# A selective scan over 24-slot passes: skip products behind the side jobs, copies of y a slot later, and a backward convolution ahead of the sums

## The chip, the cores and the metric

One core of a Trainium2 chip runs the whole program. The metric is device time in microseconds. The kernel before was run three times, with a median of 18989.68 us.

## The reference

The model has two layers over x, 16 images of 192 channels and 56 x 56 = 3136 positions. Each layer adds its branch to x: `x = x + branch(gn(x))`. The first is a bidirectional RWKV recurrence and isn't touched. The second, where the change is, is a bidirectional selective scan:

```python
def _branch(x, conv_w, conv_b, W_xproj, W_dt, dt_bias, A_log, D):
    xc = silu(conv_b + sum((xp[:, k:k + L, :] * conv_w[:, k] for k in range(4))))
    dbl = xc @ W_xproj.T
    dt = softplus(dbl[..., :12] @ W_dt.T + dt_bias)
    Bc, Cc = dbl[..., 12:28], dbl[..., 28:]
    A = -exp(A_log)
    # h = h * exp(dt * A) + (dt * x) * B;  y = sum over the 16 states of h * C;  + x * D
    return _selective_scan(xc, dt, Bc, Cc, A, D)

x, z = layernorm(tok) @ W_in_x.T, layernorm(tok) @ W_in_z.T      # 192 -> 384 channels
y_f = _branch(x, forward weights)
y_b = _branch(x[:, ::-1, :], backward weights)[:, ::-1, :]
out = ((y_f + y_b) * silu(z)) @ W_out.T + b_out
```

All is float32. The skip term is `x * D` in the scan.

## The kernel before, in words

A loop runs over the 16 images. Each round has one block for the first layer and one for the second, and only the second matters here.

**Tiling.** The 3136 positions are cut into seven chunks of 448. The second layer goes over them forwards (passes 0 to 6) and then backwards (passes 7 to 13); the 384 channels are three groups of 128 (`e` or `k` = 0, 1, 2), and the 16 states are taken in eight pairs (`p` = 0 to 7). One slot is one pair of one group, so a pass has 24 slots and an image 336. In a slot `q` these instructions carry the recurrence:

- ScalarE makes the decays exp(dt * A) in PSUM (L1410, twice), sets the state between the two halves (L1419) and keeps the carried state (L1427).
- VectorE (odd pairs, L1252) or GpSimd (even pairs, L1471) makes the input products du * B.
- VectorE scans (L1263).
- GpSimd multiplies the scan's output by C (L1479). Its results lie in a ring of four buffers, and the output product of slot q waits until the sum of slot q - 4 is done. The scan's results lie in a ring of three, and the scan of slot q waits for the output product of slot q - 3.
- TensorE adds the products up into y, in one PSUM bank (`YBANK`): in each odd slot the sums of two slots (L1157, four matmuls), two slots behind the scan. The first matmul into y of each group is the skip product `skipd` (L1149), which starts the accumulation anew, so the former y must have been read by then (`y_free`).

y is read by a copy on ScalarE in forward passes (`ye`, L1375; SyncE then stores it in DRAM, `ys`, L1561) and by a product with the gate on VectorE in backward passes (`ye`, L1239). In backward passes L1152 adds the stored forward y.

**Side jobs.** What prepares the next pass runs in the gaps: the normalization (`ns`, `n1`, `n2`, `nm`), the projection (`x` on TensorE, L1081, copied by ScalarE, `xe`, L1329), the causal convolution (`cv`, four matmuls, L1095), its silu in four steps on ScalarE (`c1` to `c4`: L1336, L1341, L1345, L1349) with the last product on VectorE (`xc`, L1226), the projections `xp` (L1102) and `t` (L1107, step size; read by L1363 on ScalarE), and in backward passes the gate (`z`, L1112, read by L1382 and released by `z4`, L1399) and the output projection (`o`, L1134, read by `ou`, L1244). `dp` (L1062) spreads du for VectorE's products.

**What sets the order.** `side_schedule` writes for each engine a list of times in slots, one for each side job; sorted by time, they give the order. An engine does the side jobs of slot g (those with time below g + 1) at the end of its slot g. The times only order the work within an engine; what makes engines wait is semaphores. For a backward pass the convolutions have the times `1.3, 6.0, 10.7` after `t = PER * (i - 1) - 2.5`, so that of group 0 falls in slot 22 of pass i - 2, group 1's in slot 3 (3.5) and group 2's in slot 8 (8.2). The preparation of pass i lies in the slots of pass i - 1; passes 6 to 12 prepare the seven backward ones.

The same function gives each TensorE job one of the banks 6 and 7 (`WBANK`), the one that is released first by the times:

```python
b = banks[k % len(banks)] if t < -10 else min(banks, key=lambda n: until.get(n, -99))
until[b] = release[name, i, e]
jobs[name, i, e] = (k, b, used.get(b, 0))
```

A job waits until all former uses of its bank are released (`w.wait_ge(c_wf[b], n)`). With this rule the convolutions of groups 0 and 1 of a backward pass follow one another on the same bank (pass 10: both bank 7, uses 55 and 56; pass 11: both bank 6, uses 59 and 60). A convolution's bank is released by `xc` (L1226) on VectorE, for group 0 in slot 3 (3.4), behind the scan and the input product of that slot. The banks are the same before and after the change.

TensorE's main loop has, in each slot, first the skip product (if the slot begins a group), then the sums (if it is odd), then the side jobs.

Of the kernel before, what the change touches and what calls it, by code (L numbers as in the profile page):

```python
# [24 lines left out]
Q = NI * PER  # L25
CHUNK = [(0, c) for c in range(NC)] + [(1, c) for c in reversed(range(NC))]
# [13 lines left out]
NXC, NDT, NDU, NR2 = 5, 3, 3, 3  # L40
# [24 lines left out]
def side_schedule():  # L65


    pe, act, dve, pool, sp = [], [], [], [], []

    def conv(i, e, t):  # L70
        if (i, e) == (0, 0):
            dve.append((t, "cd", i, e))
        else:
            pe.append((t, "cv", i, e))
        act.extend([(t + 1.9, "c1", i, e), (t + 2.6, "c2", i, e), (t + 3.2, "c3", i, e), (t + 3.9, "c4", i, e)])
        dve.append((t + 4.6, "xc", i, e))

    def step_size(i, e, t):
        pe.append((t, "t", i, e))
        act.extend([(t + 1, "t1", i, e), (t + 2, "t2", i, e), (t + 2.6, "t3", i, e)])  # L80
        dve.append((t + 2.9, "td", i, e))
        pool.append((t + 3.9, "du", i, e))
        pe.append((max(NP * (EJ * i + e) - 2, t + 4.5), "dp", i, e))
        o = max(t + 3.4, NP * (EJ * i + e - 2) - 0.5 if i else t)
        sp.extend([(o, "dd", i, e), (o + 0.02, "de", i, e), (t + 5 if i or e else o + 0.01, "ud", i, e)])

    def project(i, t, u, v):

        pe.append((t, "xp", i, 0))
        act.append((t + v, "p1", i, 0))  # L90
        sp.append((t + 1.5, "cw", i, 0))
        for e in range(EJ):
            step_size(i, e, t + u[e] if i or not e else (-1.9, 1)[e - 1])
        for G in range(4):
            r = PER * i - NP + 2 * G if i else -100
            if i:
                sp.extend([(max(r + 1, t + 2), "bl", i, G), (max(r + 3, t + 2.1), "cl", i, G)])
            else:
                sp.extend([(t + (5.3 if G else 2) + G, "bl", i, G), (t + 5.9 + G, "cl", i, G)])

    def gate(i, e, t):
        pe.append((t, "z", i, e))
        act.extend([(t + 2, "z1", i, e), (t + 2.7, "z2", i, e), (t + 3.3, "z3", i, e), (t + 4, "z4", i, e)])
        pool.append((t + 4.8, "g", i, e))

    for i in range(NI):
        s = CHUNK[i][0]
        t = PER * (i - 1) - 2.5 * (i > 1) if i else -60
        if not s:
            act += [(t - 1.7, "ns", i, 0)]  # L110
            dve += [(t + 1.0, "nc", i, 0)]
            pe += [(t - 0.2, "n1", i, 0), (t + 2.1, "n2", i, 0)]
            act += [(t + 1.9, "nq", i, 0), (t + 3.0, "nr", i, 0), (t + 4.6, "xh", i, 0)]
            if i:
                pool += [(t + 3.4, "nm", i, 0)]
            else:
                dve += [(t + 1.9, "nq", i, 0), (t + 3.4, "nm", i, 0)]
            sp += [(t + 5, "nw", i, 0), (t + 8, "xw", i, 0)]
            for e, (u, v) in enumerate(((4.2, 6.4), (4.3, 8.6 if i > 1 else 7.4), (6.2, 11))):
                pe.append((t + u, "x", i, e))  # L120
                act.append((t + u + 1.2, "xe", i, e))
                conv(i, e, t + v)
            project(i, t + 15.6, (1.2, 1.7, 4.7), 1.2)
        else:
            sp += [(t - 8, "xl", i, 0), (t + 9, "nl", i, 0)]
            for e, v in enumerate((1.3, 6.0, 10.7)):
                conv(i, e, t + v)
            project(i, t + 15.6, (1.9, 2.3, 5.2), 1.5)
            t += 2.5
            gate(i, 0, t + 21.6)  # L130
            gate(i, 1, t + 26.4)
            gate(i, 2, t + 33.4)
            for k in range(CJ):
                o = t + 2 * PER + (6.4, 7.9)[k]
                pe.append((o, "o", i, k))
                dve.append((o + 1.5, "ou", i, k))
            sp.append((o + 2.5, "out", i, 0))
            sp.append((t + PER + 4, "yl", i, 0))
        for e in range(EJ):
            t = NP * (EJ * i + e + 1) + LAG - 1  # L140
            if not s:
                act.append((t + 0.9, "ye", i, e))
            else:
                dve.append((t + 1.5, "ye", i, e))
        if not s:
            sp.append((t + 1.5, "ys", i, 0))
    sp += [(PER * (NC - 2) + 13, "dg", 1, 0), (PER * (NI - 2) + 13, "dg", 0, 0)]
    sp.append((PER * NC, "pl", NI - 1, 0))
    dve += [(PER * (i + 2) + 12 if i < NI - 2 else Q - 9, "st", CHUNK[i][1], 0) for i in range(NC, NI - 1)]
    dve += [(PER * 9 + 20, "st", 0, 0), (Q - 8.5, "ga", 0, 0), (Q - 6.5, "gb", 0, 0), (Q - 2.5, "gd", 0, 0)]  # L150
    pe += [(Q - 7.5, "gm", 0, 0), (Q - 4.5, "gv", 0, 0), (Q - 1.5, "gw", 0, 0), (Q + 0.2, "oa", NI - 1, 0),
           (Q + 0.3, "oa", NI - 1, 1), (Q + 9, "gk", 0, 0)]
    act += [(Q - 5.5, "gq", 0, 0), (Q - 3.5, "ge", 0, 0), (Q - 3.4, "gs", 0, 0), (Q - 0.5, "gi", 0, 0)]
    plans = [sorted(p, key=lambda a: a[0]) for p in (pe, act, dve, pool, sp)]
    jobs, used, until = {}, {}, {}
    last = dict(n1="nc", n2="nr", x="xe", cv="xc", xp="p1", t="td", z="z4", o="ou", gm="gi")
    read = {(name, i, e): t for p in plans[1:4] for t, name, i, e in p}
    release = {(name, i, e): read.get((last.get(name), i, e)) for _, name, i, e in plans[0]}
    for k, (t, name, i, e) in enumerate(a for a in plans[0] if a[1] not in ("dp", "gv", "gw", "gk", "oa")):
        banks = WBANK if t >= -10 else [*WBANK, 0, 1, 2, 3]  # L160
# [3 lines that stand above are left out]
        used[b] = used.get(b, 0) + 1  # L164
        if t < -10:
            first = dict(used)
    jobs["cv", 0, 0] = (None, DUBANK, 0)
    return plans, jobs, first
# [19 lines left out]
def build(nc, d, ctx):  # L188
    def sb(name, shape, dt=F32):
        return ctx.enter_context(nc.sbuf_tensor(name, shape, dt))  # L190
# [24 lines left out]
    skipd = sb("skipd", [128, 2, EJ, 128])  # L215
# [269 lines left out]
    def take(*shape, parts=128, phase=None):  # L485

        if phase is not None:
            at[0] += (phase - at[0]) % 4
        n = 1
        for s in shape:  # L490
            n *= s
        o = at[0]
        at[0] += n
        assert at[0] <= arena_n, at[0]
        v = arena[0:parts, o:o + n]
        if len(shape) == 2:
            v = v.rearrange("p (a b) -> p a b", a=shape[0])
        elif len(shape) == 3:
            v = v.rearrange("p (a b c) -> p a b c", a=shape[0], b=shape[1])
        return v  # L500
# [19 lines left out]
    ys = take(NU, T)  # L520
# [431 lines left out]
    xc = take(NXC, T, phase=0)  # L952
# [47 lines left out]
    def freed(w, name, i, e=0):  # L1000

        _, b, k = jobs[name, i, e]
        w.wait_ge(c_wf[b], k + 1)
# [30 lines left out]
    def y_free(w, r):  # L1034

        w.wait_ge(c_ya, min(r, EJ * NC))
        w.wait_ge(c_yv, r - EJ * NC)

    def layer1_tensor(e):
        w = Waits(e)  # L1040
# [100 lines left out]
        for g in range(-2, Q + LAG):  # L1141
            q = g - LAG
            if 0 <= q < Q:
                r, i, k, p, s = pair(q)
                y = ps[:, YBANK, 0:T]
                if p == 0:
                    y_free(w, r)
                    freed(w, "cv", i, k)
                    e.matmul(y, skipd[:, s, k, :], xc[:, r % NXC, :], start=True, stop=False)  # L1149
                if s and p == NP - 1:  # L1150
                    w.wait_ge(s_yl[i % 2], 16 * ((i - NC) // 2 + 1))
                    e.matmul(y, ident[:, :], yf[:, k, :], start=False, stop=False)  # L1152
                if p % 2:
                    w.wait_ge(c_mc, q + 1)
                    for a in range(2):
                        for h in range(2):
                            m = e.matmul(ps[64 * h:64 * h + 64, YBANK, 0:T], rep[:, 0:64],  # L1157
                                         pr[:, (q - 1 + h) % NPR, a * T:a * T + T], start=False,
                                         stop=p == NP - 1 and a == 1)
                            if a:  # L1160
                                m.then_inc(c_sm, 1)
            side(g)
        side(Q + 200)

    def layer1_vector(e):
# [501 lines left out]
```

## Time and profile before

| what | us |
|---|---|
| median of three runs | 18989.68 |
| lowest and highest | 18980.05, 19108.81 |
| the profiled execution | 19009.29 |
| its span, first to last instruction | 19007.5 |

Mean granted clock of TensorE: 0.885 of full speed. The trace is one execution. L12 is line 12 of the kernel, the idle time of an instruction is that of its engine just ahead of it, and the releaser is what the semaphores show as the last thing it waited for. All rows below are of the ninth image; the other fifteen repeat it closely.

### The profile page before, as it was taken

What the parts mean: (1) busy time and instruction counts of PE and PEld (TensorE: products, weight loads), DVE (VectorE), ACT (ScalarE), POOL (GpSimd) and SP (SyncE); (2) the same over time, 40 slices, a digit from 0 to 9 for tenths busy, and PEclk for the clock granted to TensorE, in tenths of its full rate; (3) what the DMA queues carried; (4) which work ended last, traced back from release to release, by engine and by line L of the source; (5) the groups of instructions that cost most, each with busy time, mean ns of one, the idle gap of its engine ahead of it and who ended that gap; (6) DMA issues with size and microseconds to landing.
All of it is one profiled execution on the core that took longest, in us unless ns stands there. A gap on an engine that the chain in (4) does not pass through costs nothing. (4 is left out here: it accounts for less than half of the span.)

```text
span 19007.5 us, 189410 instructions
## 1 busy us (share of the span) xinstructions
PE 15391.1 (81%) x45218; PEld 5361.0 (28%) x45218; DVE 17199.8 (90%) x13477; ACT 13152.4 (69%) x33212; POOL 16875.4 (89%) x11028
## 2 busy tenths in 40 slices
PE   7887888878888788887888878878788887888878
PEld 2222222322223222222222222222222222222222
DVE  7989989899898998989989899898998989989899
ACT  6767767677676776767767677676776767767676
POOL 6979979799797997979979799797997979979799
PEclk8988888888888888888888898888888889888888
DMA  2424424244242442424424244242442424424243
GB/s 74 121 60 114 120 63 120 60 115 119 67 118 61 114 117 67 118 66 112 114 67 118 66 116 110 67 118 65 114 113 67 119 68 116 108 68 121 70 117 103
DMA packets 880507, 1820.79 MB, mean 96 GB/s; under 512 B 189546, under 2 KB 595012, under 8 KB 879236
## 3 DMA queue, kind: packets, MB, share of 16 engines
q1 hardware_dynamic: 879236, 1807.12, 36.5%
q8 instruction: 398, 6.52, 0.1%
q14 instruction: 873, 7.15, 0.1%
HBM read 1083.80 MB, written 245.63 MB: 70 GB/s over the span
## 5 line engine op out<-in xcount | busy, mean ns | idle before, releaser
L1263 DVE TENSOR_TENSOR_SCAN arena<-ps,arena 128x897 f32<-128x897 f32 x5376 | 10993.9, 2065 | 521.1 <-ACT arena L1427 265.9
L1479 POOL TENSOR_TENSOR arena<-arena 128x896 f32<-128x896 f32 x5376 | 9418.8, 1769 | 311.2 <-DVE arena L1263 279.0
L1410 ACT ACTIVATE ps<-arena,A 128x448 f32<-128x448 f32 x10752 | 6390.9, 627 | 2360.2 <-DVE arena L1263 2277.1
L1157 PE MATMUL ps<-arena,rep 128*64 128x448 f32 x21504 | 5489.8, 641 | 1473.0 <-POOL arena L1479 1463.8
L1471 POOL TENSOR_TENSOR arena<-arena 128x896 f32<-128x896 f32 x2688 | 4770.4, 1775 | 202.5 <-DMA arena<-arena 131.4
L1252 DVE TENSOR_TENSOR arena<-ps,arena 128x896 f32<-128x896 f32 x2688 | 2867.0, 1067 | 69.3 <-PE ps L1062 63.3
L1157 PEld LDWEIGHTS ps<-arena,rep 128*64 128x64 f32 x21504 | 1484.1, 154 | 5086.2 <-POOL arena L1479 2720.6
L1095 PE MATMUL ps<-arena,diag 128*128 128x448 f32 x5248 | 2177.1, 559 | 77.6 <-DVE arena L1226 77.6
L1149 PE MATMUL ps<-arena,skipd 128*128 128x448 f32 x1344 | 823.7, 700 | 767.5 <-DVE arena L1239 645.7
L1095 PEld LDWEIGHTS ps<-arena,diag 128*128 128x128 f32 x5248 | 980.9, 194 | 1255.6 <-issue 1057.8
L1460 POOL TENSOR_TENSOR arena<-arena 128x448 f32<-128x448 f32 x672 | 656.3, 982 | 512.8 <-DVE arena L1232 512.8
L1427 ACT ACTIVATE arena<-arena 128x2 f32<-128x2 f32 x5376 | 1022.6, 190 | 40.9 <-DVE arena L1263 40.9
L1107 PE MATMUL ps<-arena,wdt 13*128 13x448 f32 x1344 | 751.5, 666 | 306.7 <-DVE arena L1232 295.2
L1419 ACT ACTIVATE arena<-arena 128x1 f32<-128x1 f32 x4608 | 867.8, 188 | 0.0
L1062 PE MATMUL ps<-arena,rep 64*128 64x448 f32 x1344 | 720.1, 618 | 151.1 <-DVE arena L1252 94.1
L922 POOL TENSOR_TENSOR arena<-arena 128x448 f32<-128x448 f32 x336 | 350.9, 1044 | 529.1 <-DVE arena L698 492.4
L1226 DVE SCALAR_TENSOR_TENSOR arena<-ps,vece,arena 128x448 f32<-128x448 f32 x672 | 449.7, 669 | 300.3 <-ACT arena L1349 300.3
L1336 ACT ACTIVATE arena<-ps,vece 128x448 f32<-128x448 f32 x672 | 420.9, 626 | 412.6 <-PE ps L1095 410.8
L308 PE MATMUL ps<-x,ws 96*128 96x448 f32 x1348 | 657.7, 624 | 45.7 <-DVE arena L714 45.6
L1081 PE MATMUL ps<-arena,wx 96*128 96x448 f32 x1344 | 590.8, 580 | 126.2 <-POOL arena L1454 115.9
L727 DVE TENSOR_TENSOR_SCAN ps<-ps,arena 128x898 f32<-128x898 f32 x336 | 680.3, 2025 | 11.9 <-ACT ps L885 10.3
L1112 PE MATMUL ps<-arena,wz 96*128 96x448 f32 x1344 | 668.4, 626 | 0.0
(181 smaller groups left out, 18857.7 us busy)
## 6 DMA issues: line engine op xcount, KB each, us to landing
arena<-bc_rows SPq DMA_DIRECT2D x3584, 224.0 KB, 4.5
arena<-arena SPq DMA_DIRECT2D x4160, 112.0 KB, 3.4
x_projected<-arena SPq DMA_DIRECT2D x112, 672.0 KB, 3.5
y_forward<-arena SPq DMA_DIRECT2D x112, 672.0 KB, 5.6
arena<-x_projected SPq DMA_DIRECT2D x112, 672.0 KB, 4.8
arena<-y_forward SPq DMA_DIRECT2D x112, 672.0 KB, 6.1
x<-in_x SPq DMA_DIRECT2D x120, 336.0 KB, 3.6
x_normed<-arena SPq DMA_DIRECT2D x112, 336.0 KB, 4.9
```

Of the source, the lines that this page charges most:

```text
L1062: e.matmul(ps[:, DUBANK, 0:T], rep[64:128, :], du[64:128, r % NDU, :], start=True, stop=True).then_inc(c_dp, 1)
L1095: m = e.matmul(o, diag[:, k, q, :], xh[i % 2][:, k, h:h + T], start=q == 0, stop=q == 3)
L1107: e.matmul(o, wdt[s][:, k * 128:(k + 1) * 128], res[0:R + 1, :], start=True, stop=True).then_inc(c_wt, 1)
L1149: e.matmul(y, skipd[:, s, k, :], xc[:, r % NXC, :], start=True, stop=False)
L1157: m = e.matmul(ps[64 * h:64 * h + 64, YBANK, 0:T], rep[:, 0:64], pr[:, (q - 1 + h) % NPR, a * T:a * T + T], start=False, stop=p == NP - 1 ...
L1252: e.tensor_tensor(two(bb[:, q % NB, :]), ps[:, DUBANK, 0:T].unsqueeze(1).to_broadcast([128, 2, T]), br[:, p - 1:p + 1, :], ALU.mult).then_ ...
L1263: e.tensor_tensor_scan(rev(hh[:, q % NH, 0:W2], s), rev(decays(q)[:, 0:W2], s), rev(bb[:, q % NB, 0:W2], s), car[:, 2 * k + p % 2, n:n + 1 ...
L1410: e.activation(two(decays(q))[:, a, :], dt2[:, r % NR2, p % 2, :], ACT.Exp, scale=Am[s][:, 2 * k + p % 2, n:n + 1]).then_inc(c_ex, 1)
L1419: e.activation(bb[:, q % NB, T:T1], car[:, 2 * k + p % 2, n:n + 1] if i % NC else zero[:, 0, 0:1], ACT.Copy).then_inc(c_rs, 1)
L1427: e.activation(car[:, 2 * k + p % 2, n:n + 2], h[:, 0:T1 + 1:T1] if s else h[:, T - 1:W2:T1], ACT.Copy).then_inc(c_ca, 1)
L1471: e.tensor_tensor(two(bb[:, q % NB, :]), du2[:, r % NR2, :].unsqueeze(1).to_broadcast([128, 2, T]), br[:, p:p + 2, :], ALU.mult).then_inc( ...
L1479: e.tensor_tensor(pr[:, q % NPR, :].rearrange("p (a b) -> p a b", a=2), two(hh[:, q % NH, :]), cr[:, p - p % 2:p - p % 2 + 2, :], ALU.mult ...
```

## The change

There are three parts.

1. The copy of y in forward passes and its store stand one slot later (`ye` from t + 0.9 to t + 1.9, `ys` from t + 1.5 to t + 2.5). The copy of x of group 2 (`xe`) and the first silu step of group 0 (`c1`) go one slot later with it.
2. TensorE's skip product, with its wait for y and for `xc`, stands at the end of its slot, behind the side jobs.
3. The backward convolution of group 1 has the time 2.8 in place of 3.5: slot 2, and so, by part 2, ahead of the skip product of slot 2 and of the sums of slot 3.

```diff
         else:
-            pe.append((t, "cv", i, e))
-        act.extend([(t + 1.9, "c1", i, e), ...
+            pe.append((t - 0.7 * (CHUNK[i][0] and e == 1), "cv", i, e))
+        act.extend([(t + 1.9 + 0.25 * (i > 0 and not CHUNK[i][0] and not e), "c1", i, e), ...
...
-                act.append((t + u + 1.2, "xe", i, e))
+                act.append((t + u + (2.2 if i and e == 2 else 1.2), "xe", i, e))
...
-                act.append((t + 0.9, "ye", i, e))
+                act.append((t + 1.9, "ye", i, e))
...
-            sp.append((t + 1.5, "ys", i, 0))
+            sp.append((t + 2.5, "ys", i, 0))
...
                 y = ps[:, YBANK, 0:T]
-                if p == 0:
-                    y_free(w, r)
-                    freed(w, "cv", i, k)
-                    e.matmul(y, skipd[:, s, k, :], xc[:, r % NXC, :], start=True, stop=False)
...
             side(g)
+            if 0 <= q < Q and p == 0:
+                y_free(w, r)
+                freed(w, "cv", i, k)
+                e.matmul(y, skipd[:, s, k, :], xc[:, r % NXC, :], start=True, stop=False)
```

TensorE, slots 2 to 5 of a backward pass, before. `wz` is the gate's product z, `diag` the convolution, `rep` the sums, `skipd` the skip product; c_ybwd is counted up by L1239, c_mulc by GpSimd's output products, c_free6 and c_free7 by the readers of the banks.

```order
L1149 MATMUL ps<-arena,skipd 128x448 [waits c_ybwd]
L1112 MATMUL ps<-arena,wz 128x448 [waits c_free6]
L1112 MATMUL ps<-arena,wz 128x448
L1157 MATMUL ps<-arena,rep 64x448 [waits c_mulc]
L1157 MATMUL ps<-arena,rep 64x448 x3
L1095 MATMUL ps<-arena,diag 128x448 [waits c_free7]
L1095 MATMUL ps<-arena,diag 128x448 x3
L1157 MATMUL ps<-arena,rep 64x448 [waits c_mulc]
L1157 MATMUL ps<-arena,rep 64x448 x3
```

The same place after the change (the lines of the sums and of the skip product have other numbers there, L1153 and L1162):

```order
L1112 MATMUL ps<-arena,wz 128x448 [waits c_free6]
L1112 MATMUL ps<-arena,wz 128x448
L1095 MATMUL ps<-arena,diag 128x448 [waits c_free7]
L1095 MATMUL ps<-arena,diag 128x448 x3
L1162 MATMUL ps<-arena,skipd 128x448 [waits c_ybwd]
L1153 MATMUL ps<-arena,rep 64x448 [waits c_mulc]
L1153 MATMUL ps<-arena,rep 64x448 x3
L1153 MATMUL ps<-arena,rep 64x448 [waits c_mulc]
L1153 MATMUL ps<-arena,rep 64x448 x3
```

The convolution has gone ahead of the skip product and of the first sums, and the skip product behind z.

ScalarE, slots 9 and 10 of a forward pass, before. L1375 is the copy of y, L1410 the decays, L1349 the last silu step of group 1, L1336 the first of group 2.

```order
L1345 ACTIVATE arena<-arena 128x448 [waits c_cexp]
L1375 ACTIVATE arena<-ps 128x448 [waits y_stored,c_sum]
L1410 ACTIVATE ps<-arena,A 128x448 [waits c_scan]
L1410 ACTIVATE ps<-arena,A 128x448
L1419 ACTIVATE arena<-arena 128x1 [waits c_carry]
L1427 ACTIVATE arena<-arena 128x2
L1349 ACTIVATE arena<-arena 128x448 [waits c_cln]
L1336 ACTIVATE arena<-ps,vece 128x448 [waits c_du,c_job]
```

The same place after:

```order
L1345 ACTIVATE arena<-arena 128x448 [waits c_cexp]
L1410 ACTIVATE ps<-arena,A 128x448 [waits c_scan]
L1410 ACTIVATE ps<-arena,A 128x448
L1419 ACTIVATE arena<-arena 128x1 [waits c_carry]
L1427 ACTIVATE arena<-arena 128x2
L1349 ACTIVATE arena<-arena 128x448 [waits c_cln]
L1336 ACTIVATE arena<-ps,vece 128x448 [waits c_du,c_sum,c_job]
L1375 ACTIVATE arena<-ps 128x448 [waits y_stored,c_sum]
```

The copy has moved behind the next decays and both silu steps. The orders of VectorE and GpSimd don't change. On SyncE the store of y goes behind one other store in each forward pass.

## Rows read from the trace of the kernel before

**Rows 1.** Windows, passes 3, 10, 12: us; busy (count) PE, PEld, DVE, ACT, POOL; PEclk; DMA

```profile
9951.41:10019.22 67.81, 55.13 (x161) 18.23 (x160) 64.56 (x45) 50.20 (x132) 66.87 (x42) 0.86 0.43 113
...
10427.10:10498.49 71.39, 59.27 (x175) 20.76 (x174) 67.04 (x51) 51.00 (x134) 67.66 (x43) 0.88 0.44 113
...
10568.38:10636.62 68.24, 56.58 (x176) 19.02 (x174) 66.83 (x51) 50.87 (x134) 67.74 (x43) 0.90 0.48 122
```

**Rows 2.** Waits of GpSimd (total us, times, longest): passes 8 to 12, then 2 to 5

```profile
POOL arena L1479 <- DVE arena L1263: 8.7, 11, 1.4
POOL arena L1479 <- PE ps L1157: 1.6, 2, 0.8
...
POOL arena L1479 <- DVE arena L1263: 3.4, 4, 0.9
```

**Rows 3.** Timeline of pass 3, slots 9 to 12: start, us, engine, line, [idle before]

```profile
9978.36 1.72 PE L1157 MATMUL ps<-arena,rep 128*64 128x448 f32 x8
...
9980.16 0.54 ACT L1375 ACTIVATE arena<-ps 128x448 f32<-128x448 f32 x1 [3.71 <-PE ps L1157]
...
9982.50 0.68 DVE L1226 SCALAR_TENSOR_TENSOR arena<-ps,vece,arena 128x448 f32<-128x448 f32 x1 [2.43 <-ACT arena L1349]
...
9985.26 1.76 POOL L1479 TENSOR_TENSOR arena<-arena 128x896 f32<-128x896 f32 x1 [0.83 <-DVE arena L1263]
...
9987.08 1.67 PE L1157 MATMUL ps<-arena,rep 128*64 128x448 f32 x4 [3.65 <-POOL arena L1479]
```

**Rows 4.** Timeline of pass 10, TensorE, slots 2 and 3

```profile
10434.69 1.86 PE L1149 MATMUL ps<-arena,skipd 128*128 128x448 f32 x2 [2.86 <-DVE arena L1239]
10436.35 3.19 PE L1112 MATMUL ps<-arena,wz 96*128 96x448 f32 x4
10439.47 2.56 PE L1157 MATMUL ps<-arena,rep 128*64 128x448 f32 x8
10441.96 3.27 PE L1095 MATMUL ps<-arena,diag 128*128 128x448 f32 x8
```

**Rows 5.** Timeline of pass 10, VectorE and ScalarE, slots 3 to 7

```profile
10437.54 0.67 DVE L1226 SCALAR_TENSOR_TENSOR arena<-ps,vece,arena 128x448 f32<-128x448 f32 x1
...
10445.27 0.64 ACT L1336 ACTIVATE arena<-ps,vece 128x448 f32<-128x448 f32 x1 [2.80 <-PE ps L1095]
...
10447.75 2.08 DVE L1263 TENSOR_TENSOR_SCAN arena<-ps,arena 128x897 f32<-128x897 f32 x1 [2.60 <-ACT arena L1427]
```

**Rows 6.** Timeline of pass 10, GpSimd: the fifth and sixth output products

```profile
10442.69 3.48 POOL L1479 TENSOR_TENSOR arena<-arena 128x896 f32<-128x896 f32 x2
```

**Rows 7.** Timeline, pass 10, slot 18; windows behind waits of 3.65, 2.86, 4.78 us

```profile
10484.40 1.86 PE L1149 MATMUL ps<-arena,skipd 128*128 128x448 f32 x2 [4.78 <-DVE arena L1239]
...
9987.00:9990.00 3.00, 2.92 (x8) 0.92 (x9) 3.00 (x2) 1.56 (x5) 3.00 (x3) 0.54 0.01 3
...
10434.60:10441.00 6.40, 6.31 (x10) 2.38 (x12) 6.40 (x6) 3.81 (x11) 6.40 (x6) 0.50 0.35 123
10484.40:10492.00 7.60, 7.60 (x16) 2.47 (x18) 6.90 (x4) 4.24 (x12) 7.60 (x7) 0.50 0.85 206
```

**Rows 8.** Timeline of pass 12, TensorE, slot 2; the window behind its wait

```profile
10575.98 1.02 PE L1149 MATMUL ps<-arena,skipd 128*128 128x448 f32 x2 [2.98 <-DVE arena L1239]
10576.83 1.67 PE L1112 MATMUL ps<-arena,wz 96*128 96x448 f32 x4
...
10575.90:10582.00 6.10, 6.02 (x19) 2.60 (x20) 6.10 (x6) 3.87 (x11) 6.10 (x5) 1.00 0.50 155
```

**Rows 9.** Timeline: passes 6 and 12, VectorE's L1226, GpSimd's fifth output product

```profile
10164.53 0.68 DVE L1226 SCALAR_TENSOR_TENSOR arena<-ps,vece,arena 128x448 f32<-128x448 f32 x1
...
10169.65 3.49 POOL L1479 TENSOR_TENSOR arena<-arena 128x896 f32<-128x896 f32 x2
...
10578.81 0.68 DVE L1226 SCALAR_TENSOR_TENSOR arena<-ps,vece,arena 128x448 f32<-128x448 f32 x1
...
10584.18 3.48 POOL L1479 TENSOR_TENSOR arena<-arena 128x896 f32<-128x896 f32 x2
```

More of the change, by code:

```diff
@@ L73, in conv @@
         else:
-            pe.append((t, "cv", i, e))
-        act.extend([(t + 1.9, "c1", i, e), (t + 2.6, "c2", i, e), (t + 3.2, "c3", i, e), (t + 3.9, "c4", i, e)])
+            pe.append((t - 0.7 * (CHUNK[i][0] and e == 1), "cv", i, e))
+        act.extend([(t + 1.9 + 0.25 * (i > 0 and not CHUNK[i][0] and not e), "c1", i, e), (t + 2.6, "c2", i, e), (t + 3.2, "c3", i, e), (t + 3.9, "c4", i, e)])
         dve.append((t + 4.6, "xc", i, e))
```

## Prediction, made before the changed kernel was run

> **What bounds the kernel now.** I read the windows view first, with image nine of sixteen cut into its 14 passes of 24 slots (at the first scan of each). A forward pass takes 67.8 us with GpSimd busy for 66.9 and VectorE for 64.6; a backward one 71.4 with 67.7 and 67.0; the last backward one that still prepares a successor 68.2 with 67.7 and 66.8 [rows 1]. So GpSimd (L1479, L1471) is packed, VectorE almost so, and no order of work takes a pass below some 67 us. The most that this change can give back is GpSimd's idle time. The waits view puts it at 10.3 us in five backward passes (8.7 for VectorE's scan, 1.6 for TensorE's sums) and 3.4 us in four forward ones, once 0.85 us in each [rows 2]. TensorE's and ScalarE's idle time counts only where one of these two waits for it.
>
> **Part 1, forward: copies of y one slot later.** The chain is read in pass 3 [rows 3]. ScalarE comes to the copy of y (L1375) and waits 3.71 us for the sums that TensorE starts at 9978.36; the decays and the last activation of the convolution (L1349) are queued behind it. VectorE therefore waits 2.43 us for L1349 before L1226, the next scan is late, and GpSimd loses 0.83 us. After the change the decays, L1349 and L1336 are ahead of the copy. The copy itself can't run before 9980.1 in either order, and its reader, the skip product, is needed only before the sums of the following odd slot. TensorE waits 3.65 us for GpSimd soon after those anyway, so the later copy is covered. The 2.43 us goes. What is late next is GpSimd itself, so each forward pass gains the 0.83, not the 2.43: 0.84 x 5 passes = 4.2 us per image. For the first pass, which starts without a predecessor and isn't in these rows, I take 1.3 us, between 0 and 4 (four such chains). The moved L1329, L1336 and the store of y on SyncE's queue (past one store of the normalized input) I cost at 0: ScalarE is idle for 17 us of each forward pass [rows 1], and the next user of the stored y comes seven slots later. If that cover were missing, a loss of up to the 0.84 of each pass would come back. Sum: -5.5 us per image.
>
> **Part 2, backward: skip product behind the side jobs.** In pass 10 TensorE waits 2.86 us for VectorE's L1239 in front of L1149, and z's products, the sums and the convolution all stand behind it; then they run with nearly doubled durations [rows 4]. ScalarE waits 2.80 us for that convolution, and the scan behind it 2.60 us [rows 5]. That stall is what opens GpSimd's idle time a few slots later. With L1149 moved, z's products (L1112) start as soon as the previous sums end, at 10431.83 (2.86 us before L1149's start), and at the full clock's 1.67 us [rows 8] are through at about 10433.5. In the second slot of this kind (a wait of 4.78 us [rows 7]) the moved step-size product frees ScalarE in the same way. GpSimd doesn't wait there, so I price this at 0, at most 0.7 us of VectorE's lead per pass.
>
> **Part 3, one backward convolution ahead of the sums.** Here the change costs. The planner gives the convolutions of channel groups 0 and 1 of a backward chunk the same bank, so group 1's must wait until VectorE's L1226 has read group 0's. That read stands in slot 3. Until now the convolution was in slot 3 too, behind the sums, and TensorE was late, so the wait hardly showed. Now it is in slot 2. In pass 10 L1226 ends at 10437.54 + 0.67 = 10438.21 [rows 5]; z's products end at 10433.5. So TensorE waits about 4.7 us, and behind the waiting matmul stand the skip product and the sums of pairs 0 and 1, which start at 10439.47 today and could start as soon as GpSimd's second output product is there. Who waits for these sums: GpSimd has four buffers for its output products, so its fifth one of the pass needs sum 0. It starts at 10442.69 [rows 6], which is 4.48 us after L1226's end.
>
> How long after L1226's end is the first sum done? At full clock: convolution 3.27 [rows 4], skip 1.02 [rows 8], sums 1.72 [rows 3], less 0.2 in which the runs overlap: 5.8 us. The clock decides the rest. After the wait of 2.86 us the granted clock was 0.50 (1.2 GHz) for 6.4 us; after the wait of 4.78 us, 0.50 for 7.6 us; after one of 3.65 us, 0.54 for 3 us; after one of 2.98 us in pass 12 it stayed at 1.00 (2.4 GHz) [rows 3, 7, 8]. The new wait of 4.7 us is near the longest of these, so I expect half clock behind it. Each us at half clock costs half a us: 3 us of it give 7.3, 5 us 8.3, 8 us 9.8. I take 5 us, the middle of what followed the two waits above 3.5 us (3 and 7.6), hence 8.3; the end at 8 us is rival D.
>
> GpSimd's fifth output product starts between 4.4 and 5.6 us after L1226's end in the seven passes 6 to 12, 4.8 in the mean; the first and the last of the seven are shown (4.44 and 4.69) [rows 9]. So GpSimd gets a new wait of 8.3 - 4.8 = 3.5 us in each of seven passes: 24.5 us per image. VectorE's lead can move L1226 ahead by some 0.3 us (its scan of slot 2 needs a GpSimd product and has little room): -2. The new wait stands ahead of the slots in which GpSimd idles now, so that idle time is absorbed, except for some 0.3 us per pass: 10.3 - 1.5 = 8.8 us go. Parts 2 and 3 together: 24.5 - 2 - 8.8 = +13.7 us per image.
>
> This rests on matmuls not overtaking one another, which the rows show in every slot. The Trainium skill (TensorE: Matmul & The Clock Gate, Step-by-step) says that only weight loads are pulled ahead, the matmuls staying in program order. If they could pass, the sums would run during the wait, and the sum would be that of rival C.
>
> **The sum.** +13.7 - 5.5 = +8.2 us per image, x 16 = +131 us. The profiled execution took 19009.29 us (its span is 19007.5), 19.6 above the median of the runs, 18989.68. Against its own time: 19140; put on the runs' median: 19120 us, 0.7% slower. A measurement of this kernel can tell about 1%.
>
> **Rivals.**
> B, the clock stays full. For it speaks pass 12 [rows 8], against it that its wait was only 2.98 us. Then 5.8 - 4.8 = 1.0 us x 7 = 7, less 2, less 8.8, less 5.5: -9.3 us per image, -149 us: 18840.
> C, the convolution's wait isn't there or isn't on GpSimd's path. What is removed counts alone: -(8.8 + 5.5) x 16 = -229 us: 18760, 1.2% faster. Against it: the bank and the rows above. For it: how far GpSimd runs ahead may shift once VectorE is relieved. If its fifth output product came 3.5 us later relative to L1226, nothing would be lost; this is the point from which C decides.
> D, half clock for the whole stretch (8 us, near the 7.6 of [rows 7]). Then 9.8 - 4.8 = 5.0 us x 7 = 35, less 2, 8.8 and 5.5: +18.7 us per image, +299 us: 19290, 1.6% slower. The skill's same page (HAM oscillation) describes this pattern, a wait in each round that makes each burst start cold. The trace agrees at 4.78 us and not at 2.98.
>
> **How the numbers follow.** Forecast 0.45 (19120), B 0.20, C 0.12, D 0.23. The range, 18890 to 19270, reaches nearly to B and to D. Faster by over 1% (below 18800): most of C, 0.10. Slower by over 1% (above 19180): D, and the upper third of the forecast's own spread (6 us at half clock instead of 5 adds 56 us), 0.37. Within 1%: 0.53.
>
> **What would show it.** Right: in passes 6 to 12 TensorE waits some 4 to 5 us before L1095 for VectorE's L1226, about 112 times; GpSimd's L1479 waits for TensorE's sums by 300 to 400 us in all; passes 6, 7 and 12 grow by 3 us each, passes 2 to 5 shrink by 0.8; ScalarE's waits at L1375 and VectorE's 2.43 us before L1226 are gone. Wrong: if passes 6 and 7, where GpSimd has no idle time to give back, keep their length, then part 3 costs nothing and C holds. If the wait before L1095 is there but the granted clock behind it is near 1, it is B.

## The result, and the profile after

| | before | after |
|---|---|---|
| device time, median of 6 runs each (us) | 19001.32 | 19174.34 |
| lowest to highest (us) | 18980.05 to 19108.81 | 19162.44 to 19180.65 |
| profiled span (us) | 19007.5 | 19172.4 |

The changed kernel is slower by 0.86% (ratio 1.0086, 95% interval 1.0073 to 1.01), 173 us. The forecast was 19120 us, the range 18890 to 19270. It stood on the first three runs of the kernel before (18989.68); of the 54 us between forecast and result 12 lie in that base and 42 in the change itself.

First the passes, from the windows view of after: image nine, passes 3, 6, 7, 10, 12 and 13, each from its first scan to the next pass's, the last to its last scan. Columns: stretch and length in us; busy time (count) of PE, PEld, DVE, ACT and POOL; granted clock; DMA share; GB/s.

```profile
10032.48:10100.05 67.57, 53.99 (x166) 18.35 (x164) 64.56 (x46) 50.69 (x132) 67.57 (x43) 0.90 0.45 114
10231.81:10296.16 64.35, 46.88 (x147) 15.47 (x146) 63.19 (x43) 46.58 (x121) 64.35 (x39) 0.89 0.45 115
10296.16:10365.03 68.87, 53.40 (x161) 18.46 (x160) 63.69 (x45) 51.20 (x135) 67.07 (x43) 0.90 0.49 125
10509.06:10579.86 70.80, 56.82 (x172) 20.05 (x170) 66.85 (x51) 51.28 (x134) 66.74 (x42) 0.90 0.44 113
10651.36:10722.95 71.59, 57.50 (x176) 19.90 (x176) 67.13 (x50) 51.20 (x134) 67.80 (x43) 0.90 0.46 117
10722.95:10790.41 67.46, 48.05 (x161) 16.02 (x160) 62.56 (x49) 40.05 (x110) 63.55 (x39) 0.80 0.20 50
```

Against [rows 1]: pass 3 has no GpSimd idle time left (67.57 of 67.57, with one instruction more in the stretch than before), while pass 12 grew from 68.24 to 71.59 with the same GpSimd work (67.74 and 67.80). Pass 10, which had idle time to give back, stayed at about 71.

Next the waits, over the whole run, of the kernel before (engine, line, what it waited for: total us, times, longest):

```profile
ACT arena L1375 <- PE ps L1157: 470.2, 187, 4.2
DVE arena L1226 <- ACT arena L1349: 300.3, 128, 4.5
POOL arena L1479 <- DVE arena L1263: 279.0, 318, 2.9
PE ps L1095 <- DVE arena L1226: 77.6, 112, 2.3
DVE x L1244 <- PE ps L1134: 36.3, 75, 1.1
POOL arena L1479 <- PE ps L1157: 21.9, 28, 0.8
```

and of the changed kernel (its sums are on L1153, not L1157):

```profile
PE ps L1095 <- DVE arena L1226: 397.6, 130, 4.7
POOL arena L1479 <- PE ps L1153: 353.6, 129, 3.9
DVE arena L1226 <- ACT arena L1349: 105.9, 48, 4.5
POOL arena L1479 <- DVE arena L1263: 92.7, 179, 2.2
ACT arena L1375 <- PE ps L1153: 87.1, 100, 1.1
DVE x L1244 <- PE ps L1134: 61.6, 32, 2.8
```

GpSimd's wait for VectorE's scan shrank by 186 us, and its wait for TensorE's sums grew by 332. The second outweighs the first. Two other rows moved: the convolution's wait for L1226 (78 to 398 us) and VectorE's for the output projection (36 to 62).

Then one place, slots 2 to 5 of pass 10. TensorE's timeline after the change, beside [rows 4]:

```profile
10511.72 1.72 PE L1153 MATMUL ps<-arena,rep 128*64 128x448 f32 x8 [1.11 <-POOL arena L1479]
10513.72 1.77 PE L1112 MATMUL ps<-arena,wz 96*128 96x448 f32 x4 [0.27 <-ACT arena L1399]
10520.22 5.78 PE L1095 MATMUL ps<-arena,diag 128*128 128x448 f32 x8 [4.73 <-DVE arena L1226]
10525.84 0.92 PE L1162 MATMUL ps<-arena,skipd 128*128 128x448 f32 x2
10526.68 3.23 PE L1153 MATMUL ps<-arena,rep 128*64 128x448 f32 x16
```

VectorE's and GpSimd's, of the same stretch:

```profile
10519.50 0.67 DVE L1226 SCALAR_TENSOR_TENSOR arena<-ps,vece,arena 128x448 f32<-128x448 f32 x1
10530.57 2.08 DVE L1263 TENSOR_TENSOR_SCAN arena<-ps,arena 128x897 f32<-128x897 f32 x1 [3.46 <-POOL arena L1479]
...
10528.57 3.49 POOL L1479 TENSOR_TENSOR arena<-arena 128x896 f32<-128x896 f32 x2 [3.90 <-PE ps L1153]
```

And the granted clock behind that wait (windows view, columns as above):

```profile
10520.00:10525.00 5.00, 4.78 (x7) 2.30 (x8) 5.00 (x4) 2.89 (x8) 4.67 (x3) 0.50 0.02 7
10525.00:10529.00 4.00, 4.00 (x19) 1.50 (x19) 2.11 (x2) 2.96 (x8) 0.43 (x1) 0.96 0.02 4
```

The reader sees one chain. z's products end at 10515.5. TensorE waits 4.73 us for L1226, which ends at 10520.17. The convolution then takes 5.78 us where [rows 4] had 3.27, since the clock is at 0.50 (1.2 GHz); the clock is back near 2.4 GHz only from 10525 on. The sums stand behind it, GpSimd's fifth output product waits 3.90 us for the first of them, and VectorE's next scan 3.46 us for GpSimd. From the end of L1226 to the fifth product it is 10528.57 - 10520.17 = 8.4 us.

### The profile page after: what moved, and what is told of

Its sections match the earlier page's. It is cut to its first block and busy times, and to the rows that moved or that the text cites. A ratio compares the mean times of both kernels' runs of the same rounds, so it can differ in the third digit from the quotient of the medians.

```text
span 19172.4 us, 189410 instructions
## 1 busy us (share of the span) xinstructions
PE 15559.6 (81%) x45218; PEld 5442.1 (28%) x45218; DVE 17204.9 (90%) x13477; ACT 13215.8 (69%) x33212; POOL 16867.6 (88%) x11028
## 5 line engine op out<-in xcount | busy, mean ns | idle before, releaser
L1479 POOL TENSOR_TENSOR arena<-arena 128x896 f32<-128x896 f32 x5376 | 9421.5, 1773 | 448.5 <-PE ps L1153 353.6
L1410 ACT ACTIVATE ps<-arena,A 128x448 f32<-128x448 f32 x10752 | 6396.1, 627 | 2979.8 <-DVE arena L1263 2895.4
L1153 PE MATMUL ps<-arena,rep 128*64 128x448 f32 x21504 | 5400.8, 631 | 1554.5 <-POOL arena L1479 1551.9
L1153 PEld LDWEIGHTS ps<-arena,rep 128*64 128x64 f32 x21504 | 1458.7, 151 | 5126.3 <-POOL arena L1479 2606.4
L1095 PE MATMUL ps<-arena,diag 128*128 128x448 f32 x5248 | 2402.3, 606 | 397.6 <-DVE arena L1226 397.6
L1095 PEld LDWEIGHTS ps<-arena,diag 128*128 128x128 f32 x5248 | 1072.3, 212 | 1697.7 <-issue 1185.4
L1162 PE MATMUL ps<-arena,skipd 128*128 128x448 f32 x1344 | 804.0, 685 | 501.8 <-DVE arena L1239 262.3
L1460 POOL TENSOR_TENSOR arena<-arena 128x448 f32<-128x448 f32 x672 | 659.1, 988 | 514.6 <-DVE arena L1232 514.5
L1107 PE MATMUL ps<-arena,wdt 13*128 13x448 f32 x1344 | 705.2, 629 | 261.8 <-DVE arena L1232 250.3
L922 POOL TENSOR_TENSOR arena<-arena 128x448 f32<-128x448 f32 x336 | 337.1, 1003 | 503.6 <-DVE arena L698 456.2
L1336 ACT ACTIVATE arena<-ps,vece 128x448 f32<-128x448 f32 x672 | 422.4, 629 | 515.3 <-PE ps L1095 511.8
L1081 PE MATMUL ps<-arena,wx 96*128 96x448 f32 x1344 | 655.0, 633 | 146.3 <-POOL arena L1454 137.0
L727 DVE TENSOR_TENSOR_SCAN ps<-ps,arena 128x898 f32<-128x898 f32 x336 | 680.1, 2024 | 11.9 <-ACT ps L885 10.3
L826 ACT ACTIVATE arena<-ps 128x448 f32<-128x448 f32 x336 | 181.9, 541 | 715.5 <-PE ps L310 220.2
L933 POOL TENSOR_TENSOR arena<-arena 128x448 f32<-128x448 f32 x336 | 349.6, 1040 | 361.0 <-ACT arena L872 360.9
```

Of the source, the lines that this page charges most:

```text
L1095: m = e.matmul(o, diag[:, k, q, :], xh[i % 2][:, k, h:h + T], start=q == 0, stop=q == 3)
L1107: e.matmul(o, wdt[s][:, k * 128:(k + 1) * 128], res[0:R + 1, :], start=True, stop=True).then_inc(c_wt, 1)
L1410: e.activation(two(decays(q))[:, a, :], dt2[:, r % NR2, p % 2, :], ACT.Exp, scale=Am[s][:, 2 * k + p % 2, n:n + 1]).then_inc(c_ex, 1)
L1479: e.tensor_tensor(pr[:, q % NPR, :].rearrange("p (a b) -> p a b", a=2), two(hh[:, q % NH, :]), cr[:, p - p % 2:p - p % 2 + 2, :], ALU.mult ...
```

## The experiments

Theory A says that the loss is part 3's wait for the shared bank, with all that is queued behind it. Its rivals say that another part brings it, or that the wait alone costs and the clock is a side effect. Each variant was run beside fresh runs of the kernel before, whose medians were 18999 to 19017 us, so the ratios compare variants better than the times do. Lengths below are means over 16 images from scan to scan, summed over passes; "rest" is from an image's last scan to the next image's first. The table is of one execution of each kernel; those of part 1 and of part 2 alone took 56 and 33 us more than the medians of their kernels (3.5 and 2.0 us per image).

| us per image | before | after | parts 1+2 | part 3 | part 1 | part 2 | dummies | last pass | early release |
|---|---|---|---|---|---|---|---|---|---|
| passes 0 to 5 | 418.7 | 411.7 | 411.9 | 420.8 | 413.2 | 419.9 | 412.0 | 412.2 | 412.3 |
| pass 6 | 64.4 | 64.2 | 64.4 | 64.7 | 64.4 | 64.8 | 64.2 | 64.2 | 64.0 |
| passes 7 to 12 | 417.1 | 428.6 | 407.7 | 412.2 | 416.2 | 407.4 | 413.3 | 407.7 | 408.6 |
| pass 13 | 63.1 | 67.4 | 65.9 | 63.8 | 63.3 | 65.3 | 66.0 | 64.2 | 65.0 |
| rest | 221.6 | 223.6 | 224.1 | 221.9 | 223.5 | 226.7 | 223.5 | 224.5 | 224.2 |

**Parts 1 and 2 without part 3.** The changed kernel with the convolution back behind the sums:

```diff
-            pe.append((t - 0.7 * (CHUNK[i][0] and e == 1), "cv", i, e))
+            pe.append((t, "cv", i, e))
```

> The changed kernel with the backward convolution of group 1 back at its old time (slot 3, behind the sums); parts 1 and 2 stay. Theory A (the convolution's wait for VectorE's L1226, with the sums queued behind it, is the cost): GpSimd's wait for TensorE's sums, 353.6 us in the changed kernel, falls below 60; passes 8 to 12 lose most of the idle time that they had before; the forward passes keep their gain of some 6.9 us per image; pass 13 stays slow. In all 8 to 10 us per image below the kernel before: 18850, ratio 0.992. Rival (part 2, the skip product behind the side jobs, is what costs, and the convolution's place is harmless): the time stays within 40 us of the changed kernel, 19170, ratio 1.009.

Measured: 18835.3 us, ratio to before 0.9911 (0.9894 to 0.9927). The waits that answer:

```profile
PE ps L1095 <- DVE arena L1226: 81.5, 114, 0.9
POOL arena L1479 <- DVE arena L1263: 75.2, 121, 2.3
DVE x L1244 <- PE ps L1134: 42.0, 27, 2.8
POOL arena L1479 <- PE ps L1153: 17.3, 22, 1.4
```

GpSimd's wait for the sums is gone (353.6 to 17.3 us). On top of parts 1 and 2, part 3 costs 339 us, 20.9 us of each image in passes 7 to 12 (332 us by the ratios). That is theory A; how much of it goes by way of the clock is left to the dummies below.

**Part 3 alone**, in the kernel before:

```diff
-            pe.append((t, "cv", i, e))
+            pe.append((t - 0.7 * (CHUNK[i][0] and e == 1), "cv", i, e))
```

> The kernel before with the convolution alone moved to slot 2. The skip product still stands ahead of it and waits for y, so the convolution's own wait for L1226 is short. Theory A: the sums still come behind the convolution, some 2 us late for GpSimd in the passes where the clock is at half, but ScalarE's wait for the convolution shrinks in return: within 60 us of the kernel before, 18940 to 19060. Rival (moving it costs by itself, whatever stands ahead of it): as much as in the changed kernel without its forward gain, 19250 or more.

Measured: 18987.18 us, 0.9989 (0.9979 to 0.9999). GpSimd's wait for the sums is 59.9 us and the longest wait before the convolution 2.6 us. With the skip product still in front, TensorE reaches the convolution too late for the bank to be a long wait. Passes 7 to 12 even shrink by 4.9 us per image, while passes 0 to 5, where the edit does nothing, came out 2.1 longer. So parts 2 and 3 are not additive: the loss is theirs together. They were not run together without part 1, but part 1 alone (next) changes passes 7 to 12 by only -0.9 us per image, and on top of it parts 2 and 3 cost 290 us.

**Part 1 alone**: the four time edits (`c1`, `xe`, `ye`, `ys`) in the kernel before.

```diff
-                act.append((t + 0.9, "ye", i, e))
+                act.append((t + 1.9, "ye", i, e))
...
-            sp.append((t + 1.5, "ys", i, 0))
+            sp.append((t + 2.5, "ys", i, 0))
```

> The kernel before with the copies of y, the store and the two steps that go with them one slot later; TensorE's order as before. Theory A: the forward gain belongs to this part alone, VectorE's 300 us before L1226 fall below 50 and passes 1 to 5 shrink by 1.1 to 1.7 us each, 6.9 us per image: 18890, ratio 0.994. Rival (the forward gain needs the skip product moved as well): less than 40 us below the kernel before.

Measured: 18884.29 us, 0.9928 (0.991 to 0.9946). Passes 1 to 5 lose 6.0 us per image. The wait of L1226 for L1349 did not fall below 50 us as expected, but only to 105.9 (48 times). The 80 that went are five per image. The three per image that remain stand in the stretch ahead of pass 0 (6.6 us in image nine, before and after alike), where the change has no edit.

**Part 2 alone**: the skip product behind the side jobs of its slot, in the kernel before.

```diff
-                if p == 0:
-                    y_free(w, r)
-                    freed(w, "cv", i, k)
-                    e.matmul(y, skipd[:, s, k, :], xc[:, r % NXC, :], start=True, stop=False)
...
+            if 0 <= q < Q and p == 0:
+                y_free(w, r)
+                freed(w, "cv", i, k)
+                e.matmul(y, skipd[:, s, k, :], xc[:, r % NXC, :], start=True, stop=False)
```

> The kernel before with the skip product behind the side jobs; all times as before. Theory A: passes 8 to 12 lose 8 us of GpSimd's idle time per image in all, pass 13 grows by 4 us, since TensorE finishes early there, waits longer and then runs the output projection at half clock, and forward passes stay: 18940 to 18990, ratio 0.997 to 1.000. Rival (the growth of pass 13 comes from the convolution's move as well): pass 13 stays at 63 us and the time falls to 18870.

Measured: 18961.81 us, 0.9977 (0.9967 to 0.9987). Passes 7 to 12 shrink by 9.7 us per image, but pass 13 grows by 2.2 (4 was expected) and the rest by 5.1, so that little is left.

**Dummies in the wait.** The changed kernel, with matmuls that nobody reads (L736, into y's bank ahead of the skip product) between z's products and the waiting convolution, so that TensorE is busy during the wait. This is to take the clock away from the loss and leave the order; the wait for y now stands ahead of the convolution too, in front of the dummies.

```diff
+                    if i > NC and k == 1:
+                        y_free(w, EJ * (i - 1))
+                        busy(e, 5, YBANK)
```

> The changed kernel with five dummy matmuls (384 columns each, into y's bank once y has been read, overwritten by the skip product) ahead of the moved convolution in passes 7 to 12. They fill TensorE's wait for L1226 and take nothing from the wait itself. Theory A (5.8 us at full clock plus half of the us at half clock): the granted clock behind the wait is near 1, the first sum is done some 2.4 us earlier, GpSimd's wait for the sums falls from 353.6 to some 120 us, and the time to 18950 to 19000. Rival (the wait alone costs, the clock is a side effect): GpSimd still waits over 300 us and the time stays within 40 us of 19170.

Measured: 18907.08 us, 0.9948 (0.9931 to 0.9964), better than expected. TensorE's timeline, pass 10:

```profile
10379.64 5.18 PE L736 MATMUL ps<-skipd,ident 128*128 128x384 f32 x10 [1.16 <-DVE arena L1242]
10384.66 3.17 PE L1098 MATMUL ps<-arena,diag 128*128 128x448 f32 x8
```

In this pass the dummies outlast the wait: L1229 (the former L1226) ends at 10383.16, 1.50 us before the convolution starts. In most of the 96 cases the convolution starts within 0.1 us of it. The waits that answer (its lines are three further down):

```profile
POOL arena L1482 <- PE ps L1156: 108.7, 118, 2.7
...
PE ps L1098 <- DVE arena L1229: 13.6, 32, 0.4
```

The convolution stands in the same place and takes 3.17 us instead of 5.78. GpSimd's wait for the sums falls from 353.6 to 108.7 us, and 267 us of the time come back (262 by the ratios). From the end of L1229 to the fifth output product it is now 6.0 us in the mean of the 96 cases, where the changed kernel took 8.3. So of the 339 us that part 3 costs on top of the others, some 72 remain when TensorE is kept busy in the wait, a part of them by the dummies that outlast it; the other 267 go with the half clock behind it. Neither the wait alone nor the clock alone is the loss.

**The last pass as before.** Parts 1 and 2, with the skip product of pass 13 ahead of the sums as before:

```diff
+                if p == 0 and i == NI - 1:
+                    y_free(w, r)
+                    freed(w, "cv", i, k)
+                    e.matmul(y, skipd[:, s, k, :], xc[:, r % NXC, :], start=True, stop=False)
...
-            if 0 <= q < Q and p == 0:
+            if 0 <= q < Q and p == 0 and i < NI - 1:
```

> Parts 1 and 2 without the moved convolution, and in pass 13 alone the skip product ahead of the side jobs as before. Theory A (in pass 13 the earlier skip lets TensorE run ahead, wait longer and fall to half clock just before the output projection): pass 13 goes from 65.9 back to some 63.2 us, VectorE's waits at L1244 shrink, 2.7 us per image less than with parts 1 and 2: ratio to the kernel before 0.989, 18795. Rival (pass 13 grows because it starts with GpSimd further behind): it stays at 65 to 66 us, ratio 0.991.

Measured: 18806.66 us, 0.9896 (0.9879 to 0.9912). Pass 13 falls from 65.9 to 64.2 us, not to the 63.2 that were expected. In the stretch from 10 to 25 us of pass 13 the clock is at half for 1.6 us in the mean of 16 images, where parts 1 and 2 had 7.3, and VectorE's wait for the output projection there (24.6 us in all) is gone. The 1.1 us over the kernel before stay open, so the rival may have a share in them. The intervals overlap with those of parts 1 and 2, so the gain in time, 29 us, is within what the runs tell apart; pass 13's 1.6 us per image (26 us in all) agrees with it. Pass 13 itself, slots 3 to 6, first as it is with parts 1 and 2:

```profile
10538.64 1.02 PE L1162 MATMUL ps<-arena,skipd 128*128 128x448 f32 x2 [0.99 <-DVE arena L1239]
10539.59 1.72 PE L1153 MATMUL ps<-arena,rep 128*64 128x448 f32 x8
10545.51 3.25 PE L1153 MATMUL ps<-arena,rep 128*64 128x448 f32 x8 [4.19 <-POOL arena L1479]
```

and with the skip product ahead (the pass begins at 10530.50 above, at 10526.16 here):

```profile
10539.04 1.72 PE L1157 MATMUL ps<-arena,rep 128*64 128x448 f32 x8
10541.16 1.72 PE L1157 MATMUL ps<-arena,rep 128*64 128x448 f32 x8 [0.39 <-POOL arena L1483]
```

The second sums start 15.0 us into the pass in both (in all 16 images), because GpSimd's product sets them. The first ones end 3.8 us later in the second, so the wait is 0.39 us instead of 4.19, and the sums take 1.72 us instead of 3.25. TensorE was early, waited, and worked on at half clock.

**The bank released earlier.** The changed kernel with group 0's L1226 moved from slot 3 to slot 2 on VectorE, which ends the wait earlier and leaves the convolution in front of the sums:

```diff
-        dve.append((t + 4.6, "xc", i, e))
+        dve.append((t + 4.6 - 0.6 * (CHUNK[i][0] and e == 0), "xc", i, e))
```

> The changed kernel, all three parts, with VectorE's product of group 0 (L1226, which releases the bank) one slot earlier in backward passes, directly behind the product with the gate. Theory A (what costs is TensorE's wait for this release, not the convolution's place ahead of the sums): the release comes some 3 us earlier, TensorE's wait before L1095 falls below 1.5 us each, the clock stays up, GpSimd's wait for the sums falls from 353.6 to below 80 us, and the time is that of parts 1 and 2 alone, 18820 to 18880, ratio 0.991. Rival (a convolution ahead of the sums costs wherever its bank comes from): 19100 or more.

Measured: 18822.18 us, 0.9902 (0.9885 to 0.9918). TensorE's timeline, pass 10:

```profile
10328.95 4.97 PE L1095 MATMUL ps<-arena,diag 128*128 128x448 f32 x8 [1.76 <-DVE arena L1226]
10333.75 0.92 PE L1162 MATMUL ps<-arena,skipd 128*128 128x448 f32 x2
```

This pass is one of the slow cases. Of the 96 convolutions in passes 7 to 12, 93 wait, 1.3 us in the mean and 1.76 at most, and 85 take about 3.3 us; 11 take 4.7 to 5.0. In pass 10 of the first image the same wait is followed by a fast one:

```profile
947.61 3.27 PE L1095 MATMUL ps<-arena,diag 128*128 128x448 f32 x8 [1.76 <-DVE arena L1226]
```

So the waits below 1.5 us and the full clock that were expected hold for most of the passes, not for all. GpSimd's wait for the sums is 22.2 us in the whole run. The order "convolution, skip product, sums" costs nothing that the runs can tell if the bank is free soon enough, even with a short wait in front. One VectorE instruction, a slot earlier, is worth 352 us to the changed kernel, twice what it had lost against before. The place of the convolution is then worth nothing that the runs can tell either: a ratio of 0.9902 against 0.9911 without it, with intervals that overlap.

**All three parts, early release, last pass as before**, the edits of the last two together.

> All three parts, the bank released a slot earlier, and the last pass's skip product ahead of the side jobs. Theory A (once the wait is gone, the convolution's place is worth nothing either way, since GpSimd is packed in passes 7 to 12): within 20 us of parts 1 and 2 with the last pass as before, which had a ratio of 0.9896: 0.989 to 0.991. Rival (the convolution ahead of the sums is worth something by itself): ratio below 0.988.

Measured: 18816.58 us, 0.9895 (0.9879 to 0.9912). It is level with the version without part 3 (18806.66). Both beat the kernel before and the changed one; they can't be told apart.

## Why the prediction was right, and where its steps were not

The verdict held: slower, within 1%, by the mechanism named, and 54 us short of the median; against its own base the forecast was +131 us and the result +173. Point by point, with the changes in us per image read from the table and its passes:

**Part 3's wait** was predicted at about 4.7 us; it is 3.1 to 4.6 us in the mean of each of the passes 7 to 12, at most 4.7. It was claimed 112 times and is there 96 times. From L1226's end to the fifth output product I had 5.8 us at full clock plus half of 5 us at half clock, 8.3 us. Measured: 8.3 us in the mean of 96, with 4.9 us at half clock in the 8 us behind the wait; and 5.90 in most of the passes with the dummies, at full clock. That the 5 us were hit so closely is luck: they were the middle of 3 and 7.6, and the rows gave no reason for 5 rather than 3 or 8. Without part 3 the fifth product starts 5.0 us after L1226's end (4.8 assumed), so the 0.3 us by which L1226 was to come earlier hardly show. GpSimd's new wait for the sums came to 332 us (claimed 300 to 400), 3.5 us in each of the 96 passes. The Trainium skill (TensorE: Matmul & The Clock Gate, HAM oscillation) tells of a wait in each round after which each burst starts cold. The trace agrees, in all six passes, though only the first 3.9 to 5.5 us (means of each pass) of the burst ran at 0.50, which is why it was the forecast and not rival D.

**"In each of seven passes"** is the step that failed. The price of 3.5 us holds for six: 20.9 us between parts 1 and 2 and after, over passes 7 to 12. Passes 7 and 12 grew by 2.8 us each, as claimed (3). Pass 6 kept its length (64.4 to 64.2), where the text had it grow by 3 and named unchanged passes 6 and 7 as a sign for rival C. The convolutions of groups 0 and 1 of pass 7, which pass 6 prepares, have different banks: 6 (use 38) and 7 (use 40). I had carried over to all seven, and written of every backward pass ahead of the prediction, what the banks of passes 10 and 11 show. The trace of pass 6 after the change shows the convolution without a wait, ahead of L1226:

```profile
10236.52 3.27 PE L1095 MATMUL ps<-arena,diag 128*128 128x448 f32 x8
...
10241.72 0.68 DVE L1226 SCALAR_TENSOR_TENSOR arena<-ps,vece,arena 128x448 f32<-128x448 f32 x1
```

**The absorbed idle time**, 8.8 us in passes 8 to 12: in the mean of 16 images GpSimd was idle there for 9.7 us before (10.3 in image nine), and of its waits for the scan 0.7 are left after. Part 2 alone takes 9.7 us out of passes 7 to 12. With the new wait both are in one sum: +11.5 us measured for passes 7 to 12, where six times 3.5, less 2, less 8.8 gives +10.2.

**Forward**: -7.0 us instead of -5.5. Passes 1 to 5 gave 6.9 instead of 4.2. The image that I read was not the mean one: GpSimd's idle time in passes 1 to 5 was 6.3 us per image in the mean of 16, with single waits for the scan of up to 2.9 us, and 0.4 are left after. That accounts for 5.8 of the 6.9. So "the other fifteen repeat it closely", ahead of the prediction, doesn't hold here: pass 3 took 67.8 us in image nine and 68.3 in the mean. All five waits of L1226 for L1349 per image went (80 of 128 in the run), and ScalarE's at L1375 fell from 470 to 87 us, where I had them gone. Pass 0 gave 0.1 instead of 1.3.

**Pass 13 and the rest of the image** were not in the sum at all. Pass 13 grew by 4.3 us. TensorE's timeline there, first before, then after:

```profile
10646.67 1.73 PE L1157 MATMUL ps<-arena,rep 128*64 128x448 f32 x8
10650.80 1.72 PE L1157 MATMUL ps<-arena,rep 128*64 128x448 f32 x8 [2.41 <-POOL arena L1479]
10653.40 2.50 PE L1134 MATMUL ps<-arena,wout 128*96 128x448 f32 x6
```

```profile
10732.41 1.72 PE L1153 MATMUL ps<-arena,rep 128*64 128x448 f32 x8
10737.95 3.25 PE L1153 MATMUL ps<-arena,rep 128*64 128x448 f32 x8 [3.82 <-POOL arena L1479]
10742.92 4.58 PE L1134 MATMUL ps<-arena,wout 128*96 128x448 f32 x6
```

The skip product no longer holds TensorE up, its wait for GpSimd grows from 2.41 to 3.82 us, and behind it the output projection takes 4.58 us instead of 2.50. In VectorE's order L1244 stands right there:

```profile
10747.55 0.68 DVE L1244 SCALAR_TENSOR_TENSOR x<-ps,bout,x 96x448 f32<-96x448 f32 x1 [2.79 <-PE ps L1134]
```

The windows view has the clock at 1.00 in the ten us of before and at 0.54 in the eleven of after:

```profile
10650.00:10660.00 10.00, 9.13 (x31) 3.30 (x32) 9.77 (x7) 6.11 (x18) 10.00 (x7) 1.00 0.01 2
```

```profile
10736.00:10747.20 11.20, 9.25 (x16) 2.79 (x16) 8.12 (x5) 7.04 (x19) 11.20 (x8) 0.54 0.01 2
```

Parts 1 and 2 without part 3 bring 2.7 of the 4.3 us. The traces of the two kernels show where the other 1.6 come from. With all three parts each of the 16 images has 10.2 us at half clock in the stretch from 10 to 25 us of pass 13, and L1244 waits 2.8 us in each. With parts 1 and 2 seven images do (65.9 to 67.5 us long, waits of 2.4 to 2.8), four have 6.8 us at half clock (65.1 long, a wait of 1.6), and five have 3.4 to 5.3 (64.7 to 64.9, no wait). Why part 3 makes it all 16 is not shown. The rest of the image, mostly the untouched first layer, grew by 2 us.

**The sum**: -7.0 (passes 0 to 5), -0.2, +11.5, +4.3, +2.0 make +10.6 us per image, some 170 us. The forecast's +8.2 had two errors that partly cancelled: a seventh pass too many (3.5), and pass 13 and the rest left out (6.3). That the forecast came so near is in part luck.

## What to carry to other kernels

A wait that is added in an in-order queue costs what stands behind it, not what waits in it: list that, and look for the one edit that shortens the wait (here the release of a bank one slot earlier was worth 352 us, twice the loss). Two edits that each help a little or do nothing alone (18962 and 18987 us here, 18999 before) can lose together, when the first removes a delay that hid the second's wait. And a rule that is worked out by a planner's table (which bank, which slot) is to be read for each pass, not for one or two.

## What the runs showed of the hardware that was not expected

- An engine that finishes earlier can end slower. In pass 13 of image nine TensorE came 3.8 us earlier to the same product of GpSimd's, and its next four matmuls (8 records) took 3.25 us instead of 1.72.
- Matmuls that compute nothing, put into a wait, gave back 267 us of 19174 (1.4%), with the order of the rest unchanged; the mean granted clock was 0.895 instead of 0.875.
- A wait of 1.76 us was followed by a convolution of 4.97 us in one image and of 3.27 in another (early release, pass 10), while one of 2.98 us left the clock at 1.00 [rows 8]. How long the wait is does not settle by itself whether the clock falls.
- The rest of the image is the same code in all kernels but takes 221.6 to 226.7 us in the mean (219.7 to 229.6 in single images). On the whole the longer ones had more of it at half clock, in all ten traces: 220.0 us with 45 us, 229.6 with 67. What starts them so differently was not settled; in part 2 alone it is 5.1 us per image in the one execution that was profiled (33 us above the median), more than half of what passes 7 to 12 gain there.
